# Both layer norms as ScalarE activations, roundings and one split spread over three engines, and stages A and C placed anew

## The chip, the cores and the metric

The kernel runs on one core of one Trainium2 chip. The metric is device time in microseconds (us) of one execution. The core has five engines that matter here: TensorE (matmuls and transposes), VectorE, ScalarE, GpSimd, and SyncE (SP), which only issues DMAs. Each has its own in-order instruction queue; they wait for one another through semaphores.

## The reference

One transformer layer on x of shape (4, 2048, 256), fp32: local causal attention with a window of 64 keys and 16 heads of 16, then a feed-forward with ternary weights.

```
layernorm(x) = (x - mean(x)) / sqrt(var(x) + 1e-5)
q, k, v = layernorm(x) @ Wq.T, @ Wk.T, @ Wv.T
scores  = q k^T / 4, key j seen by query i if i - 64 < j <= i
x = x + (softmax(scores) v) @ Wo.T
Q(W)    = clip(round(W / (mean|W| + 1e-5)), -1, 1)
x = x + relu(layernorm(x) @ Q(W1).T + b1) @ Q(W2).T + b2
```

## The kernel before

The 8192 tokens are worked in 16 chunks of 512. Matmuls take fp16 operands; a value that needs more precision is kept as a high half (the value rounded to fp16) and a low half (the value minus its high half), and the product is summed from the parts. In names a last `h` or `l` is the half. The high half is usually rounded by ScalarE and the low half subtracted by VectorE, both reading PSUM.

A chunk's attention is 16 units `n` of 4 x 32 queries for 4 heads, 256 units in all. One unit goes through the engines so: `scores` (TensorE, a mask matmul and 8 matmuls into one of three banks), `biggest` (VectorE, negated row maximum `negm`, L567), `exps` (ScalarE, four exponentials of 96 columns with their sums, L401), `inverse` (VectorE, `rden`), `norm` (GpSimd, `p` times `rden`, L312), `turn` (VectorE, transpose into `pt`, L580), `high` (ScalarE, `th` from `pt`, L410), `low` (GpSimd, `tl` = `pt` - `th`, L329). Four units make a group; `values` (TensorE, L821) multiplies their `th` and `tl` with the values. `o_copy` and `o_add` collect the result in `osum`, `o_split` (GpSimd) makes its halves `oT`.

Stage A makes q, k and v of the next chunk: statistics (`a_stats`), 1/sqrt (`rstd_a`, GpSimd), the norm `a_norm` (VectorE, `xnA`), transposes `a_t`, projections `a_q`, `a_k`, `a_v`. SP's DMAs then place q into a block-diagonal form `qbd`, k into `k`, v into `vb`. Stage C finishes the previous chunk: output projection `wo` with the residual, statistics, `rstd_c`, `c_norm` (`xnC`), transposes `c_t`, the feed-forward `c_f` and `c_y`, store.

Every engine runs the same loop over slots, `for n in SLOTS`; slot n issues unit n on TensorE, and the later steps of a unit one or more slots later. Tables of numbers at the file's head say in which slot each piece of stage A and C stands: an entry p of a stage A table is slot 16(c-1)+p for chunk c, of a stage C table slot 16(c+1)+p. An engine works a slot's pieces in the order in which its loop tests for them; nothing is reordered by a tool. The PSUM banks 4 to 7 go round among the pieces of A and C in slot order (`_turns`). Chunk 0 has its stage A in the negative slots. The ternary weights are made in slots 14 to 24. TensorE starts with 28 matmuls `idle` on the constant `ones`, which VectorE's `consts()` writes at slot -32.

Of the kernel before, what the change touches and what calls it, by code (L numbers as in the profile page):

```python
# [4 lines left out]
TOK, D, F = 8192, 256, 1024  # L5
# [75 lines left out]
def build(nc, x_d, wq_d, wk_d, wv_d, wo_d, w1_d, b1_d, w2_d, b2_d, identf_d, mask_d, maskf_d, out_d):  # L81
# [6 lines left out]
    with ExitStack() as ctx:  # L88
# [3 lines left out]
        def sem(name):  # L92
# [172 lines left out]
        def _(e):  # L265
# [49 lines left out]
            def o_split(c, t):  # L315
                e.wait_ge(s_osum, 4 * c + 2 * t + 2)
                if c >= 1:
                    e.wait_ge(s_c, USE[c - 1, "wo1"] + 1)
                e.tensor_copy(oT[0][:, t, :], osum[:, t, :]).then_inc(s_ohi, 1)
                e.wait_ge(s_ohi, 2 * c + t + 1)  # L320
                e.tensor_tensor(oT[1][:, t, :], osum[:, t, :], oT[0][:, t, :], ALU.subtract).then_inc(s_olo, 1)

            def low(n):
                g = n // 4
                o = slice(384 * (n % 4), 384 * (n % 4) + 384)
                e.wait_ge(s_hi, n + 1)
                if g >= 2:
                    e.wait_ge(s_pv, g - 1)
                e.tensor_tensor(tl[g % 2][:, o], pt[n % 3][:, :], th[g % 2][:, o], ALU.subtract).then_inc(s_lo, 1)  # L329

            for n in SLOTS:
# [28 lines left out]
                gg = group_at(n, PV_LAG + 2)  # L360
                if gg is not None and gg % 2:
                    o_split(gg // 4, gg % 4 // 2)

        @block.scalar
        def _(e):
# [46 lines left out]

            def a_t(c, k):
# [46 lines left out]
            for n in SLOTS:  # L460
# [27 lines left out]
                if 0 <= n - 4 < NQ:  # L488
                    high(n - 4)
# [24 lines left out]
                if 0 <= n - 1 < NQ:  # L514
                    exps(n - 1)

        @block.vector
        def _(e):
# [70 lines left out]
            def a_aggr(c):  # L589
                e.wait_ge(s_stA, 4 * c + 4)  # L590
                for t in range(4):
                    ins = e.bn_aggr(mvA[c % 2][:, t, :], stA[:, t, :])
                ins.then_inc(s_mvA, 1)

            def a_norm(c, u):
                e.wait_ge(s_rsA, c + 1)
                if c >= 1:
                    e.wait_ge(s_a, 8 * (c - 1) + 2)
                for t in (2 * u, 2 * u + 1):
                    ins = e.scalar_tensor_tensor(out=xnA[:, t, :], in0=xs[c % NX][:, t, :],  # L600
                                                 scalar=mvA[c % 2][:, t, 0:1],
                                                 in1=rstdA[c % 2][:, t:t + 1].to_broadcast([128, D]),
                                                 op0=ALU.subtract, op1=ALU.mult)
                ins.then_inc(s_xnA, 1)
# [32 lines left out]

            def residual(c, u, name):
# [5 lines left out]
            def c_stats(c, u):  # L644
# [4 lines left out]
                e.wait_ge(s_stC, 2 * h + 2)  # L649
                for t in range(2):  # L650
                    ins = e.bn_aggr(mvC[u][:, t, :], stC[:, t, :])
                ins.then_inc(s_mvC, 1)

            def c_norm(c, u):
                h = 2 * c + u
                e.wait_ge(s_rsC, h + 1)
                if h >= 1:
                    e.wait_ge(s_c, USE[(h - 1) // 2, f"t{(h - 1) % 2}"] + 1)
                for t in range(2):
                    ins = e.scalar_tensor_tensor(out=xnC[:, t, :], in0=xs[c % NX][:, 2 * u + t, :],  # L660
                                                 scalar=mvC[u][:, t, 0:1],
                                                 in1=rstdC[u][:, t:t + 1].to_broadcast([128, D]),
                                                 op0=ALU.subtract, op1=ALU.mult)
                ins.then_inc(s_xnC, 1)
# [13 lines left out]
            for n in SLOTS:  # L678
# [14 lines left out]
                if 0 <= n - 1 < NQ:  # L693
                    biggest(n - 1)
# [4 lines left out]
                gg = group_at(n, PV_LAG + 1)  # L699
# [38 lines left out]
                for u in range(2):  # L738
                    c = stage_c(n, C_NORM[u])
                    if c is not None:  # L740
                        c_norm(c, u)
                    c = stage_a(n, A_NORM[u])
                    if c is not None:
                        a_norm(c, u)

        @block.tensor
        def _(e):
# [262 lines left out]
```

## Time and profile before

| | us |
|---|---|
| median of 3 runs | 789.22 (788.97 to 791.01) |
| profiled execution | 792.54 |
| its span, first to last instruction | 790.4 |
| mean granted TensorE clock | 0.959 |

| engine | busy us | share of the span |
|---|---|---|
| TensorE | 706.5 | 89% |
| VectorE | 697.2 | 88% |
| ScalarE | 642.1 | 81% |
| GpSimd | 574.3 | 73% |

Busy is time in which at least one instruction of the engine was under way. Instructions of one engine overlap at their ends, so the step from one start to the next is shorter than a duration. The shares are means over a start, a long steady part and a tail that differ.

### The profile page before, as it was taken

The page shows a single profiled execution, that of the slowest core. Times are in us where ns is not written, and L with a number is a line of the kernel's source. Part 1 is how long each engine was busy: PE and PEld are TensorE (multiplying, and loading weights), DVE is VectorE, ACT ScalarE, POOL GpSimd, SP SyncE. Part 2 cuts the span into 40 slices and gives each one's busy share as a digit, 9 for nine tenths or more (in the row PEclk, how much of TensorE's full clock was granted, in tenths as well). Part 3 has the DMA queues.
Part 4 walks back from the last instruction along what each step waited for, and adds up shares of the span by engine and source line. Part 5 has one row for each costly group of instructions (what it writes and reads, how often), then busy time and mean ns, then how long its engine had stood idle before and what let it go on. Part 6 is the DMA issues. An engine that isn't in the chain of part 4 may idle for free.

```text
span 790.4 us, 25091 instructions
## 1 busy us (share of the span) xinstructions
PE 706.5 (89%) x8412; PEld 598.4 (76%) x8412; DVE 697.2 (88%) x1600; ACT 642.1 (81%) x2676; POOL 574.3 (73%) x724
## 2 busy tenths in 40 slices
PE   7557679999899999998999999989999999998798
PEld 5336568878788878877788787878788787887687
DVE  5557989999999999998999999999999999997854
ACT  2468678799797979899797979989797979988732
POOL 6256687778786878878686877878786877777820
PEclk9677869999999999999999999999999999999899
DMA  4864424536263544526263553626263443524000
GB/s 134 191 96 92 60 45 32 98 37 114 44 89 72 66 105 48 108 33 101 58 93 74 62 104 30 114 46 105 55 82 85 39 94 37 101 36 69 15 28 28
DMA packets 430776, 57.69 MB, mean 73 GB/s; under 512 B 403380, under 2 KB 422198, under 8 KB 430648
## 3 DMA queue, kind: packets, MB, share of 16 engines
q1 hardware_dynamic: 416072, 44.15, 38.1%
q10 hardware_dynamic: 14576, 11.93, 5.1%
q8 instruction: 68, 1.11, 0.6%
q14 instruction: 60, 0.49, 0.2%
HBM read 12.00 MB, written 8.39 MB: 26 GB/s over the span
## 4 chain that ended last, share of the span: by engine, by line
ACT 30%; issue 22%; DVE 16%; POOL 15%; PE 12%; SPq 3%; DMA 1%; ACTq 1%; DVEq 0%; POOLq 0%
ACT p L401 19%; POOL tl L329 7%; POOL p L312 5%; ACT th L410 5%; DVE negm L567 3%; DVE xnC L660 3%; SPq L226 3%; PE ps L915 3%; PE ps L821 2%; PE ps L903 2%; DVE pt L580 2%; ACT hTh L457 2%; DVE xnA L600 2%; POOL rstdC L307 2%; ACT osum L447 2%
## 5 line engine op out<-in xcount | busy, mean ns | idle before, releaser
L401 ACT ACTIVATE p<-ps,negm 128x96 f32<-128x96 f32 x1024 | 339.9, 366 | 88.2 <-DVE negm L567 80.8
L329 POOL TENSOR_TENSOR tl<-pt,th 128x384 f16<-128x384 f32 x256 | 242.0, 945 | 94.8 <-ACT th L410 92.6
L312 POOL TENSOR_TENSOR p<-p,rden 128x384 f32<-128x384 f32 x256 | 216.8, 847 | 32.4 <-DVE rden L574 32.1
L401 ACT ACTIVATION_READ_ACCUMULATOR p<-ps,negm 128x1 f32 x1024 | 236.5, 232 | 0.0
L580 DVE STREAM_TRANSPOSE pt<-p 128x384 f32<-128x384 f32 x256 | 142.0, 555 | 10.9 <-POOL p L312 9.3
L410 ACT ACTIVATE th<-pt 128x384 f16<-128x384 f32 x256 | 143.4, 560 | 0.3 <-DVE pt L580 0.3
L567 DVE TENSOR_REDUCE negm<-ps 128x4 f32<-128x384 f32 x256 | 138.3, 540 | 1.3 <-PE ps L801 1.0
L801 PE MATMUL ps<-k,qbd 128*128 128x96 f16 x2048 | 132.5, 210 | 0.0
L801 PEld LDWEIGHTS ps<-k,qbd 128*128 128x128 f16 x2048 | 118.7, 100 | 13.7 <-issue 0.6
L821 PE MATMUL ps<-th,vb 128*128 128x96 f16 (+1 forms) x1120 | 103.0, 208 | 28.8 <-POOL tl L329 22.3
L821 PEld LDWEIGHTS ps<-th,vb 128*128 128x128 f16 x1120 | 96.8, 101 | 31.6 <-POOL tl L329 25.1
L903 PE MATMUL ps<-xTCl,w1T 128*128 128x256 f16 x512 | 98.4, 274 | 7.1 <-DVE xTCl L668 7.1
L821 PE MATMUL ps<-tl,vb 128*128 128x96 f16 (+1 forms) x1120 | 102.3, 208 | 0.0
L903 PE MATMUL ps<-xTCh,w1T 128*128 128x256 f16 x512 | 98.2, 274 | 0.0
L821 PEld LDWEIGHTS ps<-tl,vb 128*128 128x128 f16 x1120 | 96.4, 101 | 0.0
L675 DVE SCALAR_TENSOR_TENSOR hTl<-ps,hTh 128x512 f16<-128x512 f32 x128 | 85.9, 671 | 9.2 <-ACT hTh L457 8.6
L457 ACT ACTIVATE hTh<-ps 128x512 f16<-128x512 f32 x128 | 80.0, 625 | 15.1 <-PE ps L903 14.4
L796 PE MATMUL ps<-mask,identb 128*128 128x256 bf16 x240 | 66.9, 279 | 11.5 <-ACT p L401 6.1
L898 PE MATMUL ps<-ones,bp 128*128 128x256 f16 x256 | 70.1, 274 | 0.9
L915 PE MATMUL ps<-w2T,hTh 128*128 128x256 f16 x512 | 66.5, 273 | 0.0
L915 PE MATMUL ps<-w2T,hTl 128*128 128x256 f16 x512 | 66.4, 273 | 0.0
L903 PEld LDWEIGHTS ps<-xTCl,w1T 128*128 128x128 f16 x512 | 49.1, 98 | 16.4 <-DVE xTCl L668 10.5
(108 smaller groups left out, 1398.5 us busy)
## 6 DMA issues: line engine op xcount, KB each, us to landing
k<-kst SPq DMA_DIRECT2D x60, 288.0 KB, 3.8
vb<-vd SPq DMA_DIRECT2D x256, 32.0 KB, 2.5
out<-x SPq DMA_DIRECT2D x32, 256.0 KB, 2.5
qbd<-qs SPq DMA_DIRECT2D x248, 32.0 KB, 2.1
x<-in_L_attn_hidden ACTq DMA_DIRECT2D x15, 512.0 KB, 4.9
vb<-in_L_ffn_W ACTq DMA_DIRECT2D x2, 1024.0 KB, 9.4
k<-kst ACTq DMA_DIRECT2D x4, 288.0 KB, 3.7
x<-in_L_attn_hidden ACTq DMA_DIRECT2D x1, 256.0 KB, 3.5
```

Of the source, the lines that this page charges most:

```text
L312: e.tensor_tensor(p3, p3, rden[n % 4][:, :].unsqueeze(2).to_broadcast([128, 4, 96]), ALU.mult).then_inc(s_nm, 1)
L329: e.tensor_tensor(tl[g % 2][:, o], pt[n % 3][:, :], th[g % 2][:, o], ALU.subtract).then_inc(s_lo, 1)
L401: ins = e.activation(p[:, 96 * u:96 * u + 96], bank[:, 96 * u:96 * u + 96], ACT.Exp, bias=m[:, u:u + 1], accum_out=r[:, u:u + 1])
L410: e.activation(th[g % 2][:, 384 * (n % 4):384 * (n % 4) + 384], pt[n % 3][:, :], ACT.Copy).then_inc(s_hi, 1)
L457: e.activation(hT[0][:, 2 * f:2 * f + 2, :].rearrange("p a b -> p (a b)"), c_bank(c, f"f{h}{f}")[:, :], ACT.Relu).then_inc(s_chi, 1)
L567: e.tensor_reduce(negm[n % 4][:, :], sbank[n % 3][:, 0:384].rearrange("p (a b) -> p a b", b=96), AX.X, ALU.max, negate=True).then_inc(s_mx, 1)
L580: e.transpose(pt[n % 3][:, :], pr[n % 3][:, :]).then_inc(s_tr, 1)
L675: e.scalar_tensor_tensor(out=lo, in0=c_bank(c, f"f{h}{f}")[:, :], scalar=0.0, in1=hi, op0=ALU.max, op1=ALU.subtract).then_inc(s_cdv, 1)
L801: ins = e.matmul(bank[:, 96 * u:96 * u + 96], qbd[g // 2][:, g % 2, 128 * blk:128 * blk + 128], ks[g][:, m, 32 * blk:32 * blk + 96], start ...
L821: ins = e.matmul(pvbank[:, 32 * i0:32 * i1], lhs, rhs, start=(k == k0 and tt is th), stop=(k == 15), skip_group_check=True)
L903: ins = e.matmul(bank[:, o], w1T[:, k, ff], xTC[xp][:, k, :], start=False, stop=(xp + k == 2))
L915: ins = e.matmul(bank[:, o], hT[hp][:, f, t * 128:(t + 1) * 128], w2T[:, f, :], start=False, stop=(f == 7 and hp == 1))
```

## The change

The norms `a_norm` and `c_norm` move from VectorE to ScalarE: instead of (x - mean) * rstd they compute rstd * x + shift with shift = -mean * rstd, as an activation (Identity) with a scale and a bias per partition. VectorE now makes -mean and variance + eps behind the aggregation, and GpSimd makes rstd and shift. Of every 16 units, the roundings `th` of units 0, 1, 12, 13, 14 and 15 are made by GpSimd, in front of its subtraction. Of the two `oT` splits of a chunk, the first stays on GpSimd; the second is rounded by ScalarE and subtracted by VectorE. On VectorE `biggest(n)` stands in slot n behind `turn(n - 3)`; before it stood in slot n + 1 ahead of it. The tables are new, and the loop starts at slot -44. Below, after the tables, GpSimd's edits come first, then ScalarE's, then VectorE's; the edits for stage C have the same form as those for stage A.

```
-A_T, A_Q, A_K, A_V = (1, 2), (5, 14), (6, 15), (7, 13)
-A_STATS, A_RSTD, A_NORM = (-13, -12), -10, (-6, -5)
-Q_DMA, K_DMA, V_DMA, A_CARRY = (7, 16), (8, 17), 15, 3
+A_T, A_Q, A_K, A_V = (1, 2), (6, 13), (6, 14), (10, 11)
+A_STATS, A_RSTD, A_NORM = (-22, -22), -19, (-13, -13)
+Q_DMA, K_DMA, V_DMA, A_CARRY = (11, 20), (7, 19), 14, 1
...
+PV_LAG, O_ADD, O_SPLIT0, O_SPLIT1 = 8, 10, 14, 10
+ROUNDED = (0, 1, 12, 13, 14, 15)
...
             def low(n):
-                e.wait_ge(s_hi, n + 1)
-                if g >= 2:
-                    e.wait_ge(s_pv, g - 1)
+                if n % 16 in ROUNDED:
+                    e.wait_ge(s_tr, n + 1)
+                    if g >= 2:
+                        e.wait_ge(s_pv, g - 1)
+                    e.tensor_copy(th[g % 2][:, o], pt[n % 3][:, :]).then_inc(s_hp, 1)
+                    e.wait_ge(s_hp, n + 1 - rounded(n))
...
-                e.tensor_scalar(veA[:, :], mvA[m][:, :, 1], 1e-5, None, ALU.add).then_inc(s_veA, 1)
+                e.tensor_tensor(rstdA[m][:, :], veA[:, :], mhalf[:, :], ALU.pow).then_inc(s_powA, 1)
+                e.wait_ge(s_powA, c + 1)
+                e.tensor_tensor(shiftA[m][:, :], meanA[:, :], rstdA[m][:, :], ALU.mult).then_inc(s_rsA, 1)
...
+            def a_norm(c, u):
+                e.wait_ge(s_rsA, c + 1)
+                if c >= 1:
+                    e.wait_ge(s_a, 8 * (c - 1) + 2)
+                for t in (2 * u, 2 * u + 1):
+                    ins = e.activation(xnA[:, t, :], xs[c % NX][:, t, :], ACT.Identity,
+                                       bias=shiftA[c % 2][:, t:t + 1], scale=rstdA[c % 2][:, t:t + 1])
+                ins.then_inc(s_xnA, 1)
...
+            def o_high(c):
...
+                e.activation(oT[0][:, 1, :], osum[:, 1, :], ACT.Copy).then_inc(s_ohi, 1)
...
+                e.tensor_scalar(meanA[:, :], mvA[:, :, 0], -1.0, None, ALU.mult)
+                e.tensor_scalar(veA[:, :], mvA[:, :, 1], 1e-5, None, ALU.add).then_inc(s_mvA, 1)
-            def a_norm(c, u):
...
-                    ins = e.scalar_tensor_tensor(out=xnA[:, t, :], in0=xs[c % NX][:, t, :],
...
+            def o_low(c):
+                e.wait_ge(s_ohi, c + 1)
+                e.tensor_tensor(oT[1][:, 1, :], osum[:, 1, :], oT[0][:, 1, :], ALU.subtract).then_inc(s_olo1, 1)
...
-                if 0 <= n - 1 < NQ:
-                    biggest(n - 1)
                 if 0 <= n - 2 < NQ:
                     inverse(n - 2)
                 if 0 <= n - 3 < NQ:
                     turn(n - 3)
+                if 0 <= n < NQ:
+                    biggest(n)
```

VectorE from the program's start, before. `stA` and `mvA` are the statistics of one chunk (four instructions each), `ones` the constant that TensorE's first matmuls read.

```order
1 L520 MEMSET mhalf 128x4
2 L521 MEMSET onesf 128x128
3 L522 MEMSET ones 128x256
4 L587 BN_STATS stA<-x 128x6 x4
5 L592 BN_AGGR mvA<-stA 128x2 x4
```

The same place now:

```order
1 L640 BN_STATS stA<-x 128x6 x4
2 L647 BN_AGGR mvA<-stA 128x2 x4
3 L650 TENSOR_SCALAR meanA<-mvA 128x4
4 L651 TENSOR_SCALAR veA<-mvA 128x4
5 L573 MEMSET mhalf 128x4
6 L574 MEMSET onesf 128x128
7 L575 MEMSET ones 128x256
8 L640 BN_STATS stA<-x 128x6 x4
9 L647 BN_AGGR mvA<-stA 128x2 x4
```

The constants have moved behind the statistics of chunk 0, and those of chunk 1 follow at once.

VectorE ahead of the first maxima, before. `qs`, `kst`, `vd` are the low halves of q, k, v of chunk 0.

```order
13 L615 SCALAR_TENSOR_TENSOR qs<-ps,qs 128x512
14 L622 SCALAR_TENSOR_TENSOR kst<-ps,kst 128x512
15 L629 SCALAR_TENSOR_TENSOR vd<-ps,vd 128x8x64
16 L529 SCALAR_TENSOR_TENSOR wol<-ps,woh 128x256 x2
17 L600 SCALAR_TENSOR_TENSOR xnA<-x,mvA,rstdA 128x256 x4
18 L629 SCALAR_TENSOR_TENSOR vd<-ps,vd 128x8x64
19 L615 SCALAR_TENSOR_TENSOR qs<-ps,qs 128x512
20 L622 SCALAR_TENSOR_TENSOR kst<-ps,kst 128x512
21 L567 TENSOR_REDUCE negm<-ps 128x4 x2
```

And now:

```order
16 L662 SCALAR_TENSOR_TENSOR qs<-ps,qs 128x512
17 L669 SCALAR_TENSOR_TENSOR kst<-ps,kst 128x512
18 L582 SCALAR_TENSOR_TENSOR wol<-ps,woh 128x256 x2
19 L640 BN_STATS stA<-x 128x6 x4
20 L647 BN_AGGR mvA<-stA 128x2 x4
21 L650 TENSOR_SCALAR meanA<-mvA 128x4
22 L651 TENSOR_SCALAR veA<-mvA 128x4
23 L676 SCALAR_TENSOR_TENSOR vd<-ps,vd 128x8x64 x2
24 L662 SCALAR_TENSOR_TENSOR qs<-ps,qs 128x512
25 L669 SCALAR_TENSOR_TENSOR kst<-ps,kst 128x512
26 L620 TENSOR_REDUCE negm<-ps 128x4 x2
```

The statistics of chunk 2 now stand ahead of both `vd`, the second `qs` and `kst` and the maxima; the four `xnA` are gone from here.

ScalarE at the transposes of stage A (slots 2 to 4 of a steady chunk), before:

```order
454 L452 ACTIVATE xTCh<-ps 128x512
455 L416 ACTIVATE xTAh<-ps 128x512
456 L401 ACTIVATE p,rsum<-ps,negm 128x96 x4
457 L410 ACTIVATE th<-pt 128x384
458 L416 ACTIVATE xTAh<-ps 128x512
459 L401 ACTIVATE p,rsum<-ps,negm 128x96 x4
460 L367 DMA x<-in_L0_attn_hidden 128x4x256
461 L410 ACTIVATE th<-pt 128x384
462 L401 ACTIVATE p,rsum<-ps,negm 128x96 x4
```

And now:

```order
437 L495 ACTIVATE xTCh<-ps 128x512
438 L419 ACTIVATE p,rsum<-ps,negm 128x96 x4
439 L459 ACTIVATE xTAh<-ps 128x512
440 L419 ACTIVATE p,rsum<-ps,negm 128x96 x4
441 L459 ACTIVATE xTAh<-ps 128x512
442 L419 ACTIVATE p,rsum<-ps,negm 128x96 x4
443 L436 ACTIVATE xnA<-x,shiftA,rstdA 128x256 x4
444 L500 ACTIVATE hTh<-ps 128x512
445 L419 ACTIVATE p,rsum<-ps,negm 128x96 x4
```

The roundings `th` are gone from these slots, and the four norms of stage A stand behind the exponentials of the third.

## Rows read from the trace of the kernel before

**Rows 1.** Windows: PE, PEld, DVE, ACT, POOL busy us, granted clock, DMA share, GB/s.

```profile
55.30:128.80 73.50, 56.15 (x615) 46.10 (x614) 63.52 (x144) 57.86 (x249) 54.01 (x66) 0.78 0.37 59
128.80:674.10 545.30, 512.64 (x6370) 438.34 (x6368) 516.76 (x1195) 481.89 (x2031) 423.99 (x537) 1.00 0.47 73
```

**Rows 2.** Waits from 128.8 to 674.1 us: total us, times, longest.

```profile
ACT p L401 <- DVE negm L567: 58.5, 60, 2.9
...
PE ps L821 <- POOL tl L329: 13.6, 12, 1.1
...
PE ps L890 <- DVE xnC L660: 8.1, 11, 1.0
PE ps L903 <- DVE xTCl L668: 7.1, 12, 0.6
```

**Rows 3.** Groups by line, whole span: busy us, mean ns, idle before.

```profile
L660 DVE SCALAR_TENSOR_TENSOR xnC<-x,mvC,rstdC 128x256 f32<-128x256 f32 x64 | 55.2, 902 | 3.5 <-POOL rstdC L307 3.5
...
L574 DVE RECIPROCAL rden<-rsum 128x4 f32<-128x4 f32 x256 | 42.3, 165 | 9.5 <-ACT p L401 6.8
...
L321 POOL TENSOR_TENSOR oTl<-osum,oTh 128x512 f16<-128x512 f32 x32 | 37.0, 1157 | 2.6
L600 DVE SCALAR_TENSOR_TENSOR xnA<-x,mvA,rstdA 128x256 f32<-128x256 f32 x64 | 36.6, 614 | 1.6 <-POOL rstdA L298 1.6
...
L609 DVE TENSOR_TENSOR xTAl<-ps,xTAh 128x512 f16<-128x512 f32 x32 | 21.8, 683 | 7.0 <-ACT xTAh L416 7.0
...
L319 POOL CAST oTh<-osum 128x512 f16<-128x512 f32 x32 | 19.5, 610 | 3.8 <-DVE osum L636 3.8
```

**Rows 4.** Line L660: ns min/median/max, first and last start.

```profile
L660 DVE SCALAR_TENSOR_TENSOR xnC<-x,mvC,rstdC x64: 462/1044/1148, 107.9 to 774.0; 128x256 f32<-128x256 f32 x64
```

**Rows 5.** Timeline of ScalarE: start us, us, instruction.

```profile
8.84 0.66 ACT L385 ACTIVATE wqh<-ps 128x256 f16<-128x256 f32 x2 [5.23 <-PE ps L755]
...
438.80 0.58 ACT L410 ACTIVATE th<-pt 128x384 f16<-128x384 f32 x1
439.21 0.65 ACT L457 ACTIVATE hTh<-ps 128x512 f16<-128x512 f32 x1
...
440.92 0.34 ACT L401 ACTIVATE p<-ps,negm 128x96 f32<-128x96 f32 x1 [0.57 <-DVE negm L567]
```

**Rows 6.** Timeline of TensorE over c_f, a_q and scores.

```profile
452.27 0.27 PE L898 MATMUL ps<-ones,bp 128*128 128x256 f16 x1
...
453.37 0.59 PE L853 MATMUL ps<-xTAh,wqh 128*128 128x512 f16 x2
...
454.66 0.27 PE L796 MATMUL ps<-mask,identb 128*128 128x256 bf16 x1
...
455.11 0.27 PE L898 MATMUL ps<-ones,bp 128*128 128x256 f16 x1
```

**Rows 7.** Timelines of VectorE and TensorE at the start.

```profile
5.41 0.38 DVE L592 BATCH_NORM_AGGREGATE mvA<-stA 128x2 f32<-128x6 f32 x4
...
1.34 5.32 PE L923 MATMUL ps<-ones 128*128 128x256 f16 x28 [1.34 <-DVE ones L522]
8.39 0.63 PE L755 MATMUL ps<-identf,x 128*128 128x128 f32 x4 [1.73 <-DMA x<-in_L_attn_Wq]
```

**Rows 8.** Timelines at the start, and DMA issues: KB each, us to landing.

```profile
24.08 0.40 ACTq L367 DMA_DIRECT2D x<-in_L_attn_hidden  x1
...
29.56 22.59 SPq L226 DMA_DIRECT2D vb<-vd  x16
...
72.14 13.06 SPq L226 DMA_DIRECT2D vb<-vd  x16
...
54.09 0.24 PE L821 MATMUL ps<-th,vb 128*128 128x96 f16 x1 [6.38 <-issue]
...
x<-in_L_attn_hidden ACTq DMA_DIRECT2D x15, 512.0 KB, 4.9
```

**Rows 9.** Timeline of TensorE in the last chunk.

```profile
724.62 0.27 PE L796 MATMUL ps<-mask,identb 128*128 128x256 bf16 x1 [2.94 <-DMA k<-kst]
```

More of the change, by code:

```diff
@@ L359, in _ @@
                     norm(n - 2)
-                gg = group_at(n, PV_LAG + 2)
-                if gg is not None and gg % 2:
-                    o_split(gg // 4, gg % 4 // 2)
+                gg = group_at(n, O_SPLIT0)
+                if gg is not None and gg % 4 == 1:
+                    o_split(gg // 4)
         @block.scalar
@@ L411, in high, with c_norm @@
                              ACT.Copy).then_inc(s_hi, 1)
+            def a_norm(c, u):
[6 more added lines that the diff above has]
+                ins.then_inc(s_xnA, 1)
+            def c_norm(c, u):
+                h = 2 * c + u
+                e.wait_ge(s_rsC, h + 1)
+                if h >= 1:
+                    e.wait_ge(s_c, USE[(h - 1) // 2, f"t{(h - 1) % 2}"] + 1)
+                for t in range(2):
+                    ins = e.activation(xnC[:, t, :], xs[c % NX][:, 2 * u + t, :], ACT.Identity,
+                                       bias=shiftC[u][:, t:t + 1], scale=rstdC[u][:, t:t + 1])
+                ins.then_inc(s_xnC, 1)
+            def o_high(c):
+                e.wait_ge(s_osum, 4 * c + 4)
+                if c >= 1:
+                    e.wait_ge(s_c, USE[c - 1, "wo1"] + 1)
+                e.activation(oT[0][:, 1, :], osum[:, 1, :], ACT.Copy).then_inc(s_ohi, 1)
             def a_t(c, k):
@@ L487, in _ @@
                     load_x(c + NX)
-                if 0 <= n - 4 < NQ:
+                if 0 <= n - 4 < NQ and (n - 4) % 16 not in ROUNDED:
                     high(n - 4)
@@ L515, in _ @@
                     exps(n - 1)
+                for u in range(2):
+                    c = stage_c(n, C_NORM[u])
+                    if c is not None:
+                        c_norm(c, u)
+                    c = stage_a(n, A_NORM[u])
+                    if c is not None:
+                        a_norm(c, u)
+                gg = group_at(n, O_SPLIT1)
+                if gg is not None and gg % 4 == 3:
+                    o_high(gg // 4)
         @block.vector
@@ L649, in c_stats @@
                 e.wait_ge(s_stC, 2 * h + 2)
+                if h >= 1:
+                    e.wait_ge(s_rsC, h)
                 for t in range(2):
[L651 to L664, printed above, removed]
+                    ins = e.bn_aggr(mvC[:, t, :], stC[:, t, :])
+                ins.then_inc(s_agC, 1)
+                e.wait_ge(s_agC, h + 1)
+                e.tensor_scalar(meanC[:, :], mvC[:, :, 0], -1.0, None, ALU.mult)
+                e.tensor_scalar(veC[:, :], mvC[:, :, 1], 1e-5, None, ALU.add).then_inc(s_mvC, 1)
             def c_t(c, h):
@@ L737, in _ @@
                         c_stats(c, u)
[L738 to L744, printed above, removed]
+                gg = group_at(n, O_SPLIT1)
+                if gg is not None and gg % 4 == 3:
+                    o_low(gg // 4)
         @block.tensor
@@ L872, in wo @@
                 e.wait_ge(s_td, 8)
-                e.wait_ge(s_olo, 2 * c + 2)
+                e.wait_ge(s_olo0, c + 1)
+                e.wait_ge(s_olo1, c + 1)
                 for t in range(2):
```

72 lines of the change are left out of this document (37 added, 35 removed).

## The prediction

> **What bounds the kernel now.** I read the busy time by stretch first, then the waits of the steady stretch, then single operations, then the first 60 us in order of time.
>
> A slot is one pass of the loop, a chunk is 16 slots. By the reductions `negm` the program has three parts: the start to slot 8, a ramp with the weight preparation to slot 32, and from 128.8 us to 674.1 us twelve steady chunks; the rest is the last chunk and the tail. Twelve chunks in 545.3 us are 45.4 us each. In them VectorE is busy 516.8 us and TensorE 512.6 us, so 43.1 and 42.7 us a chunk; ScalarE has 481.9 (40.2), GpSimd 424.0 (35.3) [rows 1]. The reader is to see that no engine has much room: the best conceivable gain from moving work off VectorE ends at TensorE, 2.4 to 2.7 us a chunk below today.
>
> The waits say the same from the other side [rows 2]. TensorE waits 13.6 + 8.1 + 7.1 = 28.8 us, so its own work is (545.3 - 28.8)/12 = 43.0 us a chunk. ScalarE waits 58.5 us for `negm`, 4.9 us a chunk, so its work is 40.6. Those waits sit in the loop ScalarE - VectorE: VectorE's long norm instructions stand ahead of the maximum that ScalarE needs. VectorE is therefore what makes the others wait now, with TensorE 0.4 us behind it.
>
> **The change, part by part (per steady chunk).**
>
> *Norms to ScalarE.* VectorE loses 4 `xnC` at 902 ns and 4 `xnA` at 614 ns [rows 3]: 6.1 us by duration, some 5.7 as they overlap. The two groups have one shape and differ by half, and `xnC` alone goes from 462 to 1148 ns [rows 4]; the long ones lie beside GpSimd's work, so I read part of the 902 as the two engines disturbing one another. ScalarE gains 8 activations of 128x256 with a scale and a bias of their own per partition. No row has that form. Two plain ones of 256 columns take 0.66 us together [rows 5]: 0.38 each with 0.10 of overlap. `th` with 384 columns follows its neighbour after 0.41 where the pair's step is 0.28, about 1 ns a column [rows 5]; from 256 down to 96 columns a plain one would so come to 0.22 to 0.25, and the exponential with one pointer takes 0.34 [rows 5]. So a pointer is about 90 ns, a norm 0.38 + 0.18 = 0.56, less 0.10 overlap: 0.46 each, 3.7 us. Bounds: the pair's step of 0.28 (pointers cost nothing), 2.2 us; 0.58 (`th` in full), 4.6 us.
>
> The Trainium skill ("ScalarE: Activation LUTs", What ACT_TABLE_LOAD costs) states that each per-partition pointer operand adds about 93 ns to an ACTIVATE and that neighbours overlap by about 93 ns. This speaks against the change, and the 340 ns row agrees. By its formula a 256-column norm would be 0.585 us, 0.49 after overlap, and the eight 3.9 us instead of 3.7.
>
> *Six of sixteen roundings to GpSimd.* ScalarE loses 6 `th` at a pitch of 0.41 (438.80 to 439.21) [rows 5]: 2.5 us. GpSimd gains 6 casts of 384 columns; 512 take 610 ns [rows 3], so 0.46 each, with a wait on itself 0.55: 3.3 us (bounds 2.8 and 3.7). They fall on slots 0 to 5 of 16, which is where ScalarE gets the four `xnA` in one slot.
>
> *One split leaves GpSimd.* It loses 610 + 1157 ns = 1.8 us [rows 3]. ScalarE gains one copy, 0.48; VectorE a subtraction of 128x512. The nearest rows are 683 ns for `xTAl` [rows 3] and 1157 for the same subtraction on GpSimd; I take 0.65, with 1.2 as the upper end if it is disturbed like `xnC`. The Trainium skill ("GPSIMD Engine Reference", Specifications) states that GpSimd shares its SBUF interfaces with VectorE and contends with VectorE instructions that have two SBUF inputs. The spread of `xnC` fits it [rows 4]; by that rule the removed norms were the contended kind and the added subtraction is one too, which would put it at the upper end and the sum 0.5 us higher.
>
> *Small ones.* VectorE gains six tiny operations for -mean and variance plus eps, each no more than the 165 ns of `rden` [rows 3], and three short waits on itself: 0.5 to 1.3 us, I take 1.1. GpSimd trades its three tiny additions for three products, about even.
>
> The sums: VectorE 43.1 (by busy time; nearly all it has) - 5.7 + 0.65 + 1.1 = 39.2; ScalarE 40.6 - 2.5 + 0.5 + 3.7 = 42.3; GpSimd 35.3 + 3.3 - 1.8 = 36.8; TensorE unchanged, 43.0. So VectorE stops being the bound, TensorE becomes it, and ScalarE stands 0.7 us below it.
>
> *`biggest(n)` one slot earlier.* It now follows the transpose and stands ahead of the slot's subtractions. ScalarE needs it only at the end of the next slot, so most of the 4.9 us of wait goes. What can be late next: VectorE now waits at `biggest(n)` for `scores(n)` of the same slot, and behind it stand the slot's subtractions that free TensorE's banks. TensorE runs `scores` first in each slot, so this is covered unless the slot before was a heavy one. By the new tables slot 6 has `c_f`, `a_q`, `a_k` and scores: 1.10 + 1.29 + 1.29 + 0.45 = 4.1 us by the steps of [rows 6], slots 1 and 5 under 1.6. Added up so, every four slots TensorE has 10.0 to 10.4 and ScalarE not above 11 (an estimate), so the unevenness fits in the one slot and more by which the engines run apart.
>
> With two engines at 42.3 and 43.0 and a loop between them the period can't be 43.0. Today an engine at 43.1 beside one at 43.0 gives 45.4; I take 44.0, a gain of 1.4 us a chunk. Thirteen chunks (slots 32 to 240): -18 us. Bounds: 43.0 (-31 us) and today's 45.4 (0).
>
> *The start.* Two moves cost here. First, the statistics of chunk 0 now lie at slot -38, ahead of `consts()` at -32. TensorE's 28 idle matmuls wait for `ones`: today from 1.34 us, and they take 5.32 [rows 7]. The statistics end at 5.41 + 0.38, with the tiny ones and memsets `ones` is there at about 6.5, the idle matmuls end at 11.8, and the weights' transposes start there instead of at 8.39: +3.4 us for all behind them. Second, the statistics of chunk 2 lie at slot -6 and wait for `x2`, which ScalarE issues only at slot -1, 24.08 today [rows 8]. ScalarE now has one more rounding and some of its norms ahead of that, 1 to 2 us, so with the +3.4 the load goes out at about 29 and lands 4.9 us later [rows 8], at 34. VectorE stands until then; queued behind are the low halves of v, q and k, then the first maxima. They end at about 38.5, and the V placement starts at 37.4 instead of 29.56. It takes 22.6 us while the FFN weights load, 13.1 later [rows 8]. Behind it on SP's queue is now the second half of Q, which `scores(8)` needs: 37.4 + 20 + 3 + 2 = 62 to 64 us, where today `values(0)` started at 54.09 [rows 8]. I take +9 us at slot 8; bounds +1 (V placed in 13 us) and +12.
>
> *The ramp.* 73.5 us for 24 slots, VectorE busy 63.5 [rows 1]; it loses the norms of one to two chunks, about 6 us, and the granted clock is 0.78 there, which a denser TensorE would lift. I take -4; bounds 0 and -8.
>
> *The last chunk and tail.* Without stage A the slots are short, and the second half of K was late: 2.94 us of waiting at 724.62 [rows 9]. V is now placed from slot 12's result on instead of slot 14's, so Q and K land before slot 248. With two `xnC` off VectorE's chain: -4; bounds 0 and -8.
>
> The sum: +9 - 4 - 18 - 4 = -17 us on a span of 790.4; the profiled execution's own time is 792.5, the median of the runs 789.2, so about 3 us of it is profiling and spread. Against the median: 772.
>
> **The rivals.**
>
> *TensorE's floor is reached (0.2).* The maximum comes early enough that no wait is left: 43.0 x 13, -31, with ramp -6 and tail -5, start +7: 754. For it: ScalarE's `negm` wait, the largest of a compute engine, has one cause and that goes. Against: three engines within 4 us a chunk.
>
> *The start eats it (0.17).* Steady gain only 0.7 us a chunk (-9), start +11, ramp -2, tail -2: 787. For it: the +3.4 is certain from the order, and the `x2` wait nearly so.
>
> *ScalarE becomes the bound, slower (0.13).* Place: its in-order queue, where `exps` now also stand behind norms that need GpSimd's `shift` and behind `o_high`. If the 4.9 us of wait a chunk stay although VectorE is lighter, since they come from the loop and not from VectorE's load, its chunk is 42.3 + 4.9 = 47.2: +1.8 x 13 = +23, start +9, tail -4: 817. It decides from 3.1 us of wait a chunk upward (45.4 - 42.3). Against: in the rows the wait is for `negm` alone, and `negm` moves ahead of everything that made it late.
>
> **How the numbers follow.** Forecast 772 with 0.5 (its own range 762 to 781), the floor 754 with 0.2, the eaten gain 787 with 0.17, slower 0.13, part of it near 795. The range 752 to 790 leaves out the far slower cases and a few below. 0.3% is 2.4 us, what a measurement here can tell. Faster: 0.5 + 0.2 + 0.1 = 0.8; same 0.06 of the eaten case; slower 0.14.
>
> **What would show it.** In the changed profile: `ones` ends near 6.5 us, and the first `xTAl` is some 3.4 us late; VectorE waits about 10 us for a DMA of `x` before 35 us; eight norm activations at 0.5 to 0.6 us each; VectorE's busy share falls from 95% to about 89% in the steady stretch and ScalarE's rises from 88% to about 95%; the wait of `p` for `negm` falls below 2 us a chunk; chunk period 44. I am wrong if the period is above 45, if another wait of ScalarE replaces the one for `negm`, or if slot 8 comes no later than today.

## The result, and the profile after

| | before | after |
|---|---|---|
| median, us | 789.1 (786.94 to 791.01, 4 runs) | 753.08 (750.48 to 755.94, 4 runs) |
| ratio to before, 95% interval | | 0.9545 (0.9501 to 0.959) |
| profiled execution / its span | 792.5 / 790.4 | 754.1 / 752.3 |
| mean granted TensorE clock | 0.959 | 0.966 |

The change gains 36 us; I had forecast 17 (772, range 752 to 790). The windows of the changed kernel follow, cut where the reductions `negm` of slots 0, 8, 32 and 224 start; columns as in [rows 1].

```profile
0.00:35.60 35.60, 18.72 (x134) 13.48 (x135) 14.14 (x49) 12.97 (x28) 17.33 (x25) 0.93 0.40 111
35.60:63.00 27.40, 11.69 (x86) 7.97 (x85) 11.98 (x27) 18.13 (x80) 13.50 (x16) 0.62 0.89 156
63.00:133.20 70.20, 54.42 (x630) 45.62 (x628) 58.63 (x149) 55.47 (x235) 52.39 (x70) 0.84 0.44 63
133.20:629.50 496.30, 495.62 (x6252) 430.49 (x6249) 454.97 (x1156) 491.69 (x2030) 420.18 (x575) 1.00 0.50 79
629.50:752.30 122.80, 111.07 (x1324) 97.68 (x1319) 89.79 (x208) 88.78 (x354) 76.19 (x104) 0.99 0.26 46
```

The fourth row is the reading that matters: over twelve chunks TensorE is busy 495.62 of 496.30 us and ScalarE 491.69, both at once. Against [rows 1] (512.64 and 481.89 of 545.30) two engines are now full, not one. Cut by slots, both kernels compare so (`negm` start times read from VectorE's timeline; the period is that of slots 32 to 224, twelve chunks):

| us | slot 8 | slot 32 | slot 224 | slot 240 | end | period |
|---|---|---|---|---|---|---|
| before | 55.3 | 128.8 | 665.6 | 708.3 | 790.4 | 44.73 |
| after | 63.0 | 133.2 | 629.5 | 670.5 | 752.3 | 41.36 |

So the start costs 7.7, the ramp gives back 3.3, slots 32 to 240 give 42.2 (579.5 to 537.3) and the tail 0.3: -38.1 in all, the difference of the spans. The waits of the steady stretch, 133.2 to 629.5 us, answer to [rows 2]:

```profile
POOL tl L347 <- ACT th L428: 49.4, 73, 1.4
POOL p L323 <- DVE rden L627: 16.9, 59, 0.4
DVE rden L627 <- ACT p L419: 16.4, 36, 0.6
DVE pt L633 <- POOL p L323: 15.4, 13, 1.3
DVE oTl L687 <- ACT oTh L454: 2.0, 12, 0.2
ACT qs L466 <- PE ps L893: 1.4, 8, 0.2
PEld ps L919 <- issue: 0.9, 3, 0.3
PE ps L919 <- DVE oTl L687: 0.6, 3, 0.2
```

ScalarE's 58.5 us for `negm` are gone from the list, and TensorE's three waits of 28.8 us became one of 0.6. What waits now are mostly GpSimd and VectorE, the two engines that have room for it. The chain of work that ended last says it too:

```profile
PE 71%; ACT 10%; POOL 6%; DVE 4%; issue 4%; SPq 3%; DMA 1%; ACTq 1%; POOLq 0%; DVEq 0%
```

What the moved operations take, by line, whole span (columns as in [rows 3]), and two places of ScalarE's timeline:

```profile
L436 ACT ACTIVATE xnA<-x,shiftA,rstdA 128x256 f32<-128x256 f32 x64 | 34.2, 671 | 4.0 <-POOL shiftA L309 4.0
L446 ACT ACTIVATE xnC<-x,shiftC,rstdC 128x256 f32<-128x256 f32 x64 | 35.5, 618 | 5.3 <-POOL shiftC L318 5.3
...
L341 POOL CAST th<-pt 128x384 f16<-128x384 f32 x96 | 49.6, 517 | 0.0
...
L687 DVE TENSOR_TENSOR oTl<-osum,oTh 128x512 f16<-128x512 f32 x16 | 11.1, 692 | 2.7 <-ACT oTh L454 2.7
```

```profile
16.31 2.06 ACT L436 ACTIVATE xnA<-x,shiftA,rstdA 128x256 f32<-128x256 f32 x4
...
255.94 1.10 ACT L446 ACTIVATE xnC<-x,shiftC,rstdC 128x256 f32<-128x256 f32 x2
256.93 0.60 ACT L500 ACTIVATE hTh<-ps 128x512 f16<-128x512 f32 x1
```

Two norms take 0.99 us from the first to the start of what follows, 0.49 each.

Why `xnC` took twice as long on VectorE for some instructions as for others [rows 4] can be read off the kernel before. Two places of its timeline:

```profile
332.24 0.91 POOL L329 TENSOR_TENSOR tl<-pt,th 128x384 f16<-128x384 f32 x1
332.30 2.10 DVE L660 SCALAR_TENSOR_TENSOR xnC<-x,mvC,rstdC 128x256 f32<-128x256 f32 x2 [0.17 <-POOL rstdC L307]
...
337.37 0.86 DVE L600 SCALAR_TENSOR_TENSOR xnA<-x,mvA,rstdA 128x256 f32<-128x256 f32 x2
```

Of the 128 norms `xnA` and `xnC`, 57 start while GpSimd has a `p` or a `tl` under way; they take 1042 to 1148 ns, and 56 of them end 279 to 285 ns after that GpSimd instruction does. The 52 with no `p` or `tl` beside them take 443 to 485, and 18 of the 19 that start just ahead of one take 444 to 479. GpSimd pays too: 30 of its 256 `p` took about 1.0 us beside a norm, and in the changed kernel all 256 take 0.82 to 0.83. So the norms left VectorE with more than their own half microsecond.

The start, on VectorE, TensorE and SyncE's queue (answering to [rows 7, 8]):

```profile
6.27 0.27 DVE L575 MEMSET ones<- 128x256 f16 x1
...
31.22 1.40 DVE L640 BATCH_NORM_STATS2 stA<-x 128x6 f32<-128x256 f32 x4 [9.12 <-DMA x<-in_L_attn_hidden]
```

```profile
6.60 4.82 PE L964 MATMUL ps<-ones 128*128 128x256 f16 x28 [6.60 <-DVE ones L575]
11.26 1.04 PE L795 MATMUL ps<-identf,x 128*128 128x128 f32 x8
...
61.85 0.48 PE L833 MATMUL ps<-maskf,identb 128*128 128x384 bf16 x1 [12.30 <-DMA qbd<-qs]
```

```profile
34.53 23.07 SPq L237 DMA_DIRECT2D vb<-vd  x16
57.69 2.63 SPq L220 DMA_DIRECT2D qbd<-qs  x4
```

These are the forecast events in the forecast order: late `ones`, VectorE standing for `x2`, the placement of V behind it, and the second half of Q behind that.

### The profile page after: what moved, and what is told of

It is laid out like the page before. It is cut to its first block, busy times and chain, and to the rows that moved or that the text cites. A ratio compares the mean times of both kernels' runs of the same rounds, so it can differ in the third digit from the quotient of the medians.

```text
span 752.3 us, 25171 instructions
## 1 busy us (share of the span) xinstructions
PE 691.5 (92%) x8412; PEld 595.2 (79%) x8412; DVE 629.5 (84%) x1584; ACT 667.0 (89%) x2724; POOL 579.6 (77%) x788
## 4 chain that ended last, share of the span: by engine, by line
PE 71%; ACT 10%; POOL 6%; DVE 4%; issue 4%; SPq 3%; DMA 1%; ACTq 1%; POOLq 0%; DVEq 0%
PE ps L956 12%; PE ps L944 11%; PE ps L861 10%; PE ps L841 9%; PE ps L893 8%; PE ps L919 6%; ACT p L419 5%; PE ps L904 5%; SPq L237 3%; PE ps L939 3%; PE ps L836 3%; POOL tl L347 2%; POOL p L323 2%; PE ps L931 2%; PE ps L884 1%
## 5 line engine op out<-in xcount | busy, mean ns | idle before, releaser
L347 POOL TENSOR_TENSOR tl<-pt,th 128x384 f16<-128x384 f32 x256 | 235.4, 920 | 82.6 <-ACT th L428 74.4
L419 ACT ACTIVATION_READ_ACCUMULATOR p<-ps,negm 128x1 f32 x1024 | 247.8, 242 | 0.0
L323 POOL TENSOR_TENSOR p<-p,rden 128x384 f32<-128x384 f32 x256 | 211.5, 826 | 34.6 <-DVE rden L627 34.6
L620 DVE TENSOR_REDUCE negm<-ps 128x4 f32<-128x384 f32 x256 | 133.5, 522 | 18.1 <-PE ps L841 17.1
L428 ACT ACTIVATE th<-pt 128x384 f16<-128x384 f32 x160 | 89.6, 560 | 0.5 <-DVE pt L633 0.3
L627 DVE RECIPROCAL rden<-rsum 128x4 f32<-128x4 f32 x256 | 42.3, 165 | 30.0 <-ACT p L419 29.7
```

What stands on the lines that cost most here:

```text
L323: e.tensor_tensor(p3, p3, rden[n % 4][:, :].unsqueeze(2).to_broadcast([128, 4, 96]), ALU.mult).then_inc(s_nm, 1)
L419: ins = e.activation(p[:, 96 * u:96 * u + 96], bank[:, 96 * u:96 * u + 96], ACT.Exp, bias=m[:, u:u + 1], accum_out=r[:, u:u + 1])
L428: e.activation(th[g % 2][:, 384 * (n % 4):384 * (n % 4) + 384], pt[n % 3][:, :], ACT.Copy).then_inc(s_hi, 1)
L620: e.tensor_reduce(negm[n % 4][:, :], sbank[n % 3][:, 0:384].rearrange("p (a b) -> p a b", b=96), AX.X, ALU.max, negate=True).then_inc(s_mx, 1)
```

## The experiments

The change has three parts: P, the tables; E, the engines that do norms, roundings and the split; M, the maximum one slot earlier. Periods are of slots 32 to 224, as above. All ratios are to the kernel before, with the 95% interval. With E go its own slots of the collection and the splits (`O_ADD`, `O_SPLIT0`, `O_SPLIT1`), with P all six lines of tables. The rows of waits are from 133.2 to 629.5 us in every run, so that they compare; in this stretch the kernel before has 53.8 us of ScalarE's wait for `negm`.

### What sets the period after

**after_nobias** takes the rows that add b1 and b2 out of TensorE, 20 matmuls of 256 columns a chunk at a step of 0.109 us, 2.2 us; b1 and b2 are left out of the result.

```
-                    e.matmul(bank[:, o], bp[:, ff], ones[:, 0:256], start=True, stop=False)
...
-                e.matmul(bank[:, o], ones[:, 0:128], bp[:, F:], start=True, stop=False)
```

> The changed kernel without the 20 bias matmuls of 256 columns per chunk (b1 and b2 are left out of the result). They take 0.107 us each, 2.1 us a chunk on TensorE alone. Theory T (TensorE's columns bound the changed kernel, 41.3 us a chunk): the period falls until ScalarE binds; ScalarE's busy time is 41.0 a chunk, so at least 0.3 and at most 2.1 us a chunk, 5 to 34 us in all: 719 to 748. Rival S (ScalarE, which waits only 1.4 us in twelve chunks, is the bound): no gain in the steady part, 750 to 755.

746.46 us, 0.9441 (0.9409 to 0.9472). The period falls from 41.36 to 40.93, 0.43 of the 2.2 us taken away. In its steady stretch TensorE is busy 473.57 of 491.2 us and ScalarE 488.80. In the kernel after, then, ScalarE stands 0.4 us a chunk below TensorE (491.69 and 495.62 us in twelve), and with TensorE lighter it is the bound.

**before_nobias** is the same cut in the kernel before.

```
-                    e.matmul(bank[:, o], bp[:, ff], ones[:, 0:256], start=True, stop=False)
...
-                e.matmul(bank[:, o], ones[:, 0:128], bp[:, F:], start=True, stop=False)
```

> The kernel before without its bias matmuls (b1 and b2 are left out of the result). My prediction held VectorE to be its bound with TensorE close behind: a loss of 2.1 us a chunk on TensorE then gives 0 to 5 us, 784 to 789. Rival: the kernel before was bound by TensorE between its stalls, then 0.107 x 20 x 16 = up to 34 us, 755 to 770.

786.24, 0.9957 (0.9935 to 0.998); period 44.87, against 44.73. The period is that of the profiled execution, which was the slowest of the ten (791.84); by the medians the cut gives 3.2 us in all, 0.2 of the 2.2 us a chunk. So TensorE's own work was not the bound before.

**round0** gives all roundings back to ScalarE, 2.5 us a chunk by the 0.41 of [rows 5].

```
-ROUNDED = (0, 1, 12, 13, 14, 15)
+ROUNDED = ()
```

> The changed kernel with all 16 roundings on ScalarE again. ScalarE gains 6 x 0.41 = 2.5 us a chunk and becomes the bound under both theories. Theory T, with its slack under TensorE of 0.3 to 1: 41.3 + 1.5 to 2.2, so +24 to +35 us: 777 to 788. Rival S: the full 2.5, +40 us: 793.

784.46, 0.9927 (0.9896 to 0.9959); period 43.88, 2.5 longer: all of the added work shows in the period (theory T had 1.5 to 2.2). ScalarE is the engine that six roundings had to relieve.

**round8** gives GpSimd two more.

```
-ROUNDED = (0, 1, 12, 13, 14, 15)
+ROUNDED = (0, 1, 3, 7, 12, 13, 14, 15)
```

> The changed kernel with 8 of 16 roundings on GpSimd instead of 6 (units 3 and 7 as well). ScalarE loses 2 x 0.41 = 0.8 us a chunk, GpSimd gains 2 x 0.57 = 1.1 on 35. Theory T: nothing to gain, 750 to 756. Rival S: 0.8 us a chunk less, 13 us in all: 740.

762.81, 0.966 (0.9626 to 0.9695); period 42.09, 0.73 longer than with six. A lighter ScalarE made the kernel slower, which neither theory had; and that though GpSimd, at 430.54 of 505.1 us, is only 85% busy. Its steady waits:

```profile
POOL p L323 <- DVE rden L627: 36.5, 81, 1.0
...
PEld ps L919 <- issue: 10.6, 12, 1.0
ACT th L428 <- DVE pt L633: 9.3, 24, 0.7
PE ps L919 <- DVE oTl L687: 9.2, 12, 0.9
```

TensorE waits 0.8 us in each chunk for `oTl`, where it waited 0.6 in twelve. Slots 3 and 7 are then heavy for GpSimd with the chain `p`, `pt`, `th` behind it; that the lateness reaches `oTl` that way is read from these waits, not tested apart.

### Which part gives what

**tables_only** (P): the six lines of tables and the range of slots of the changed kernel in the kernel before.

```
-A_T, A_Q, A_K, A_V = (1, 2), (5, 14), (6, 15), (7, 13)
+A_T, A_Q, A_K, A_V = (1, 2), (6, 13), (6, 14), (10, 11)
...
-SLOTS = range(-32, NQ + 33)
+SLOTS = range(-44, NQ + 48)
```

> The kernel before with the changed tables alone, all work on its old engine. Theory T: VectorE's load stays at 42.2 us a chunk, so no gain in the steady part, and the start costs 5 to 8 us more: 788 to 800. Rival P: 765 or below.

795.91, 1.0089 (1.0067 to 1.0111), period 44.71: slower by the start (slot 8 at 63.0 us instead of 55.3), nothing in the steady part.

```profile
ACT p L401 <- DVE negm L567: 37.2, 34, 1.7
...
PE ps L878 <- POOL oTl L321: 16.3, 11, 1.5
```

**engines_only** (E and M): the changed kernel with the old tables.

```
-A_T, A_Q, A_K, A_V = (1, 2), (6, 13), (6, 14), (10, 11)
+A_T, A_Q, A_K, A_V = (1, 2), (5, 14), (6, 15), (7, 13)
```

> The changed kernel with the tables of the kernel before: norms, roundings, split and the earlier maximum as changed, every piece of stages A and C in its old slot, start included. Theory T (an engine's load and the maximum decide): most of the 3.2 us a chunk stays, and the start is 7.7 us shorter at slot 8: 745 to 760. Rival P (placement decides): the period goes back to 43.5 or more, 780 or above.

793.46, 1.0056 (1.0036 to 1.0076), period 44.64. With every operation on its new engine and the early maximum, but the old slots, nothing is gained, as the rival had it:

```profile
...
POOL rstdC L316 <- DVE veC L708: 36.8, 22, 2.9
PEld ps L861 <- POOL tl L347: 21.3, 19, 1.4
DVE pt L633 <- POOL p L323: 20.0, 33, 1.1
PE ps L861 <- POOL tl L347: 18.5, 19, 1.3
```

**big_old** (E and P): the changed kernel with the maximum where it was.

```
+                if 0 <= n - 1 < NQ:
+                    biggest(n - 1)
                 if 0 <= n - 2 < NQ:
                     inverse(n - 2)
...
-                if 0 <= n < NQ:
-                    biggest(n)
```

> The changed kernel with biggest(n - 1) at the head of slot n again, behind the subtractions of slot n - 1. The maximum is late by the one or two subtractions of 0.6 us ahead of it. Theory T: VectorE now has 3.4 us a chunk of slack, so little is lost, 753 to 760. Rival M (the earlier maximum is what removed ScalarE's 4.9 us of wait for negm): that wait comes back by at least half, 770 or above.

772.98, 0.9793 (0.9764 to 0.9823), period 42.92. My theory had 753 to 760; the rival, that the earlier maximum matters, is right. ScalarE's wait for `negm` is back, 17.7 us, and TensorE waits 10.8 for `xnC`:

```profile
ACT p L419 <- DVE negm L620: 17.7, 34, 1.0
...
PE ps L931 <- ACT xnC L446: 10.8, 11, 1.0
```

**early_only** (M): the maximum of the kernel before moved to the changed kernel's place, the reverse of that edit.

```
-                if 0 <= n - 1 < NQ:
-                    biggest(n - 1)
...
                     turn(n - 3)
+                if 0 <= n < NQ:
+                    biggest(n)
```

> The kernel before with one edit: biggest(n) in slot n behind turn(n - 3), on its old tables and engines. Theory V (VectorE's load of 42.2 us a chunk is the first limit of the kernel before): the wait of ScalarE for negm goes, but VectorE has only 2.3 us a chunk to give, and norms of up to 2 us now delay the reciprocal instead: 0.5 to 1 us a chunk, 772 to 782. Rival W (three parts that work only together: load off VectorE, early maximum, new slots): one alone gives nothing, 786 to 793.

801.54, 1.0139 (1.0107 to 1.0171), period 45.42. Taken alone, the edit that was to remove ScalarE's wait makes the kernel slower, beyond both expectations:

```profile
ACT th L410 <- DVE pt L580: 60.2, 45, 2.9
POOL veC L303 <- DVE mvC L651: 56.5, 22, 3.3
...
DVE negm L567 <- PE ps L801: 21.8, 32, 1.4
```

ScalarE's wait of 53.8 us for `negm` turned into one of 60.2 for `pt`. VectorE now stands for `scores` of the same slot, and what is queued behind comes that much later. That by itself is not the whole cause: early_tables, next, has the same wait of VectorE and is fast.

**early_tables** (M and P): the edits of tables_only and of early_only together.

```
-A_T, A_Q, A_K, A_V = (1, 2), (5, 14), (6, 15), (7, 13)
+A_T, A_Q, A_K, A_V = (1, 2), (6, 13), (6, 14), (10, 11)
...
-                    biggest(n - 1)
...
+                    biggest(n)
```

> The kernel before with the new tables and the early maximum, all work on its old engine. With tables alone the period was 44.7. Theory V: VectorE's load stays, period 43.5 or more and the start 8 us late, 775 to 790. Rival W: as tables alone, 793 to 798. If the placement and the maximum made the gain, 765 or below.

773.19, 0.9782 (0.9753 to 0.9811), period 42.96, between what the theories had.

```profile
DVE negm L567 <- PE ps L801: 19.7, 32, 0.8
...
ACT th L410 <- DVE pt L580: 7.6, 25, 0.4
```

ScalarE's wait for `pt` is down to 7.6 us, though VectorE stands for `scores` as often as in early_only and for 19.7 us instead of 21.8. What has changed is which pieces stand in the slots behind; which entry of the tables does it was not tried. Without any operation on another engine, this is 16 of the 36 us.

**engines_late** (E): the engines alone, with old tables and the old place of the maximum.

```
-A_T, A_Q, A_K, A_V = (1, 2), (6, 13), (6, 14), (10, 11)
+A_T, A_Q, A_K, A_V = (1, 2), (5, 14), (6, 15), (7, 13)
...
+                if 0 <= n - 1 < NQ:
+                    biggest(n - 1)
...
-                if 0 <= n < NQ:
-                    biggest(n)
```

> The kernel before with the engines alone changed (norms, roundings, split), old tables, the maximum late as before. With the early maximum this gave a period of 44.6. Theory V: the load is off VectorE, so 43 to 44, 765 to 785. Rival W: 790 or above.

782.43, 0.9898 (0.9869 to 0.9927), period 44.03: the load off VectorE gives 0.7 us a chunk by itself, as theory V had it (765 to 785 us).

The eight cases of the three parts:

| | neither P nor M | M | P | P and M |
|---|---|---|---|---|
| old engines, us (period) | 789.1 (44.73) | 801.5 (45.42) | 795.9 (44.71) | 773.2 (42.96) |
| new engines (E), us (period) | 782.4 (44.03) | 793.5 (44.64) | 773.0 (42.92) | 753.1 (41.36) |

Alone the parts give -0.70, +0.69 and -0.02 us a chunk, which adds to nothing; together -3.37. M costs 0.6 to 0.7 under the old tables and gives 1.6 to 1.8 under the new ones; P gives nothing or 1.1 with the late maximum and 2.5 to 3.3 with the early one. E gives 0.7 to 0.8 under the old tables and 1.6 to 1.8 under the new ones.

**norms_dve** takes back only the norms from ScalarE: VectorE computes them in their old form, with the new shift.

```
-                    ins = e.activation(xnC[:, t, :], xs[c % NX][:, 2 * u + t, :], ACT.Identity,
-                                       bias=shiftC[u][:, t:t + 1], scale=rstdC[u][:, t:t + 1])
+                    ins = e.scalar_tensor_tensor(out=xnC[:, t, :], in0=xs[c % NX][:, 2 * u + t, :], scalar=rstdC[u][:, t:t + 1],
+                                                 in1=shiftC[u][:, t:t + 1].to_broadcast([128, D]),
+                                                 op0=ALU.mult, op1=ALU.add)
```

> The changed kernel with its eight norm instructions a chunk on VectorE again (as scale times x plus shift, in the same slots), everything else as changed. VectorE gains 4 to 6 us on 37.9 a chunk (454.97/12), ScalarE loses 3.9. Theory T: VectorE at 42 to 44 becomes the bound, period 43 to 44.5, +25 to +50 us: 778 to 803. Rival P (the gain is the placement of the slots and the earlier maximum, not the norms' engine): within 8 us of 753.

787.89, 0.9979 (0.9963 to 0.9994), period 43.54, 2.2 us above the changed kernel's; nearly all of the gain is gone. In the steady part 1.2 us a chunk of it stays; what eats that is the start and the ramp, with slot 32 at 139.9 us instead of 133.2 (128.8 before). TensorE waits 15.3 us for `xnC` (row "PE ps L933 <- DVE xnC L675: 15.3, 11, 1.5"). It is slower than early_tables (42.96), which has VectorE's norms too, but every rounding on ScalarE and both splits on GpSimd. So what E changes besides the norms' engine (VectorE's six tiny operations among it) costs 0.6 us a chunk as long as the norms stay; which piece of it does was not tried.

### The start

**start_all** takes back what I had named as the start's cost: `consts()` ahead of the first statistics, `x2` loaded at slot -15 instead of -1, and chunk 0's V placed four slots later, so that the second half of Q goes first. The wait for the weights' halves that stood with the load of `x2` moves to slot 7.

```
-                if n == -32:
+                if n == SLOTS[0]:
                     consts()
...
-                if n == -1:
+                if n == -15:
+                    e.wait_ge(s_wlo, 4)
+                    load_x(2)
+                if n == 7:
                     e.wait_ge(s_wlo, 8)
-                    load_x(2)
...
-c = stage_a(n, V_DMA if n > 1 else V_DMA + 2)
+c = stage_a(n, V_DMA if n > 5 else V_DMA + 6)
```

> The changed kernel with three edits at the start only: consts() first, x2 loaded at slot -15 (once the q and k weights are transposed), and chunk 0's second half of q placed ahead of its v. Slot 8's maximum came at 63.0 us in the changed kernel. I expect ones at 1.3 instead of 6.5 us (2.9 us gained), no wait of 9 us for x2, and the wait of 12.3 us for q gone or halved: slot 8 at 50 to 54, then 4 to 5 of these us given back in the ramp if that is bound by VectorE's and ScalarE's work, and all kept if not: 741 to 748. Rival: v's placement beside the FFN weights (23 us) sets the start whatever comes before it, then 750 to 753.

742.64 (740.94 to 744.11), 0.94 (0.9376 to 0.9423), faster than both kernels. Slot 8 comes at 44.8, slot 32 at 121.8 instead of 133.2; the period is 41.36, as after. The long wait for `qbd` is gone, but `values(0)` still stands for V, whose placement takes as long as before:

```profile
28.30 21.90 SPq L237 DMA_DIRECT2D vb<-vd  x16
```

```profile
52.11 0.24 PE L863 MATMUL ps<-th,vb 128*128 128x96 f16 x1 [9.69 <-issue]
```

So 18 us earlier at slot 8 are 11.4 at slot 32: part of it is lost again on V. How much each of the three edits gives was not tried, nor whether the weight loads under way at that time are what makes this placement 22 us long and the next one 13 [rows 8].

## Why the prediction was right or wrong

**What was right.** The start: +7.7 at slot 8 against +9, with its links as forecast: `ones` at 6.6 us (6.5), transposes 2.9 us later (3.4), VectorE 9.12 us at `x2` (about 10), V placed in 23.07 us (22.6), first scores of slot 8 at 61.85 (62 to 64). That last agreement is in part luck: `x2` was issued at 26.15 us instead of about 29, so V's placement began at 34.53 instead of 37.4, and the sum had given it 20 us where its own row has 22.6 and it took 23.07. The ramp -3.3 (-4). The moved operations: ScalarE's load rose by 41.0 - 39.3 = 1.7 us a chunk, as forecast (40.6 to 42.3), and VectorE's fell by 42.2 - 37.9 = 4.3 (3.9). Their shares came out at 99% (forecast 95) and 92% (89), because the stretch itself is shorter. GpSimd's rose by 0.4 (1.5), in part because `p` and `tl` became 2 to 3% shorter each (848 to 826 ns and 942 to 920 in the mean). A norm steps at 0.49; I had 0.46.

By the formula of the Trainium skill ("ScalarE: Activation LUTs", What ACT_TABLE_LOAD costs) the estimate for such a norm was 0.585 us, and 0.49 after overlap. The trace agrees: at the start the norms take 583 to 600 ns at steps of 0.49, so this was nearer than my sum from rows.

The removed norms were disturbed by GpSimd, as the prediction had read from their spread. The Trainium skill ("GPSIMD Engine Reference", Specifications) has contention between GpSimd and VectorE instructions with two SBUF inputs, and the trace agrees with 1042 to 1148 ns for norms that start during a `p` or `tl` against 443 to 485 without one. The added subtraction did not come to its upper end of 1.2 us, since it never met the case: all sixteen `oTl` on VectorE start with no GpSimd instruction under way and take 691 to 694 ns. In fifteen of them a `tl` starts 0.46 us later, and it is the `tl` that is long, 1.00 to 1.02 us where the others take 0.91 to 0.92.

**What was wrong in size.** The steady part: -42.2 us where I had -18, and the tail -0.3 where I had -4. The mechanism was right for the change as a whole (the wait for `negm` goes, TensorE becomes the bound, ScalarE stands just under it), and two terms of the sum were mis-sized.

First, *TensorE's own 43.0 us a chunk*. Half of its error is a plain miscount: 128.8 to 674.1 holds slots 32 to 228, 12.25 chunks and not twelve. All per-chunk figures were 2% high, the period (44.5, not 45.4) as well as the load (42.2), so the difference hardly changed. (The whole chunks of slots 32 to 224 have 44.73; the light slots 224 to 228 take 8.5 us, less than a quarter of that.) The other half matters: 42.2 is the span less the labelled waits, but the changed kernel, 99.9% busy with the same matmuls, has a period of 41.36. The labelled waits fall short. In the kernel before:

```profile
303.23 0.50 PE L801 MATMUL ps<-k,qbd 128*128 128x96 f16 x8
304.87 0.19 PE L821 MATMUL ps<-th,vb 128*128 128x32 f16 x1 [1.14 <-POOL tl L329]
```

Eight matmuls of 96 columns at a step of 0.042 are issued by 303.57, so TensorE stood 1.30 us; the label has 1.14, because it counts from the modelled end of the last one. Summing, over all matmuls, the step to the next less its columns at the granted clock (a float32 transpose of 128 columns, at a step of 0.109, counted twice) gives 60.5 us over the 12.25 chunks before and 20.2 over the 12 after. The 1.7 us a chunk after are mostly no stall: most steps there are 2 to 3 ns longer than their columns, and the steps of the usual length for each form come to 41.0 us a chunk in both kernels. Counting them as TensorE's own leaves 39.9 us of stalls before, instead of the 31.7 that the rows add up to (28.8 in the three that I took). TensorE's own time is therefore 41.3, and the room below the 44.5 was 3.25 us a chunk where I saw 2.4: 0.85 x 13 = 11 us of the miss.

Second, *"the period can't be 43.0 ... I take 44.0"*, the 1.0 us of coupling. It isn't there: TensorE at 495.62 and ScalarE at 491.69 of 496.30 us run side by side and TensorE waits 0.6 us in twelve chunks. I had carried over the distance that the kernel before had from its busiest engine. That distance belonged to the order of its slots, not to having two full engines in one loop: after_nobias, with ScalarE at 488.80 of 491.2, closes up in the same way. That is 1.0 x 13 = 13 us, and with the first term's 11 the 24 us that the steady part missed. (The thirteenth chunk, slots 224 to 240, gave only 1.6 us; the twelve before it 3.37 each.)

Behind both stands a way of summing that failed: I priced the parts one by one and gave the tables a credit only where a wait of the profile named them. The eight cases show that the parts aren't additive; the tables and the early maximum are worth nothing or less each, and 1.8 us a chunk together. That they work only as a pair is shown; why is read from the waits and stays open. The wait for `negm` did not tell that, and early_only shows how little it told: the wait went and another of the same size came.

**The tail.** -4 was the credit for Q and K placed before slot 248. After slot 240 both kernels need 82 us (82.1 and 81.8). The wait of 2.94 us for `k` [rows 9] is gone, and from slot 240 to the last `negm` 39.8 us became 37.8. Behind the last `negm` 42.3 became 44.0, so the gain was given back there; what takes it was not tried.

**The rivals.** "The floor is reached" gave 754 and was right in kind (TensorE's floor is reached), but its number came out by luck, two errors against each other: -31 in the steady part (measured -42), and -11 for ramp and tail (-3.6). "The start eats it" had the start right and the steady part far too small. "ScalarE becomes the bound, slower" asked for 3.1 us of wait a chunk: none is left. A long wait of ScalarE that stays when the one for `negm` goes is seen in early_only, but there the norms are still on VectorE.

## What to carry to other kernels

When the floor is set by an engine with pipelined work, take it from the steps between its instructions, not from the span less its labelled waits; here that was 11 of the 24 us missed. Where an edit moves an engine's wait and another re-times the slots, don't add their prices: ask which instruction would be waited for next, and try the pair, since each alone measured as nothing or as a loss. Once two engines are full, giving a third more work may cost though it has room (round8).

## What was not expected of the hardware

- TensorE and ScalarE can both be over 99% busy for 496 us in a loop of in-order queues that feed one another; 0.6 us of waiting is listed for TensorE.
- An activation of 256 columns with scale and bias per partition lasts 583 to 600 ns at the start and 618 (`xnC`) and 671 (`xnA`) in the mean, but steps at 0.49 us everywhere.
- The norms that VectorE did in 902 and 614 ns [rows 3] took 549 (`xnC`) and 778 (`xnA`) in norms_dve at other places of the program. The mean depends on how many start while GpSimd has a `p` or a `tl` under way: in the kernel before such a norm takes 1042 to 1148 ns and ends, in 56 of 57 cases, 279 to 285 ns after the GpSimd instruction, against 443 to 485 ns with none beside it. Started first, the VectorE instruction keeps its time and the GpSimd one is the longer (`tl` beside `oTl`, 1.00 to 1.02 us instead of 0.91).
- The same 16 transfers `vb<-vd` take 22 to 23 us at the start and 13 to 14 at the next chunk, in before, after and start_all alike. The loads of the FFN weights are issued near the first ones; that they are the cause was not tried.
